# Interleaving 28 shared-expert units with the channel-mix steps, in a new order of TensorE's work

## The reference, cut to what matters

```
h  = layernorm(x) * (1 + ca) + sa
# time mix: h normalized again, mixed with the row before it
r, k, v = sigmoid(xr @ Wr), xk @ Wk, xv @ Wv        # 512 x 512 each
x2 = h + (r * wkv(k, v)) @ Wout
# channel mix: x2 normalized, mixed with the row before it
x3 = x2 + sigmoid(xr2 @ Wr2) * ((relu(xk2 @ Wk2) ** 2) @ Wv2)
x  = x + ga * x3
h3 = layernorm(x) * (1 + cb) + sb
shared = (silu(h3 @ Wsg) * (h3 @ Wsu)) @ Wsd        # hidden size 704
scores = softmax(h3 @ Wrouter); the best 2 of 8 experts per row
routed = sum over the two: score * (silu(h3 @ Wg[e]) * (h3 @ Wu[e])) @ Wd[e]   # hidden 352
out = x + gb * (shared + routed)
```

## Time and profile before

| | |
|---|---|
| time, three runs | 1895.73, 1896.31 (median), 1900.86 us |
| span of the profiled execution | 1895.5 us |
| PE busy | 1742.5 us, 92% of the span |
| DVE busy | 1312.1 us, 69% |
| ACT busy | 707.1 us, 37% |
| POOL busy | 619.4 us, 33% |
| DMA | 351.39 MB, mean 185 GB/s |

### The profile page before, as it was taken

The page is one execution under the profiler, slowest core; times in us unless marked ns, Lnnn a source line. Parts: engine busy times, 40 slices in busy tenths (PEclk is TensorE's granted clock), DMA queues, the critical chain, the costliest instruction groups (busy, mean ns, idle before and its releaser), DMA issues.

```text
span 1895.5 us, 29657 instructions
## 1 busy us (share of the span) xinstructions
PE 1742.5 (92%) x9060; PEld 1509.1 (80%) x9060; DVE 1312.1 (69%) x2333; ACT 707.1 (37%) x1118; POOL 619.4 (33%) x755
## 2 busy tenths in 40 slices
PE   4599999998899899997779999999999999999997
PEld 0488888886677777776678998999999999988886
DVE  4898999983798888886632227666666666655555
ACT  2344444442443434343211115454545454522222
POOL 0343333322577777776216420000000000034442
PEclk8699999999888888888798999999999999999999
DMA  8333343333855454543448735767676767666553
GB/s 332 101 116 120 120 120 120 120 99 116 299 170 183 172 190 166 187 161 128 139 167 285 260 111 199 248 228 251 228 253 225 256 221 254 229 198 178 182 181 101
DMA packets 147870, 351.39 MB, mean 185 GB/s; under 512 B 20793, under 2 KB 20793, under 8 KB 142321
## 3 DMA queue, kind: packets, MB, share of 16 engines
q1 hardware_dynamic: 117136, 263.26, 41.7%
q0 software_dynamic: 19456, 67.12, 10.8%
q10 hardware_dynamic: 11232, 20.45, 2.8%
HBM read 225.95 MB, written 124.83 MB: 185 GB/s over the span
## 4 chain that ended last, share of the span: by engine, by line
PE 72%; DVE 16%; issue 5%; DMA 3%; ACT 2%; POOL 1%; DVEq 1%; SPq 0%; ACTq 0%; POOLq 0%
PE bank L451 17%; PE bank L453 17%; PE bank L452 17%; DVE mix L1345 5%; PE bank L1828 5%; PE bank L1830 5%; PE bank L1829 5%; PE bank L462 3%; PE bank L1804 2%; DVE xh L1330 2%; DMA stage<-in_w_k 1%; DVE raw L1630 1%; DVE h_hl L1400 1%; PE bank L1758 1%; DVE raw L1625 1%
## 5 line engine op out<-in xcount | busy, mean ns | idle before, releaser
L451 PE MATMUL bank<-gu_hi,ex_x_hl 128*128 128x352 f32 x1136 | 381.6, 336 | 24.2 <-DMA ex_x_hl<-h_turned 22.3
L453 PE MATMUL bank<-gu_hi,ex_x_hl 128*128 128x352 f32 x1136 | 370.0, 326 | 0.0
L452 PE MATMUL bank<-gu_lo,ex_x_hl 128*128 128x352 f32 x1136 | 367.3, 323 | 0.0
L1541 DVE TENSOR_TENSOR hid<-bank,sg_t 128x352 f32<-128x352 f32 x142 | 74.5, 525 | 298.3 <-ACT sg_t L1071 294.5
L882 POOL DMA_DIRECT2D ex_x_hl<-h_turned x32 | 18.4, 575 | 691.1 <-PE bank L453 659.9
L451 PEld LDWEIGHTS bank<-gu_hi,ex_x_hl 128*128 128x128 f32 x1136 | 215.5, 190 | 25.2 <-issue 14.5
L1071 ACT ACTIVATE sg_t<-bank 128x352 f32<-128x352 f32 x142 | 65.9, 464 | 417.7 <-PE bank L453 390.9
L452 PEld LDWEIGHTS bank<-gu_lo,ex_x_hl 128*128 128x128 f32 x1136 | 215.6, 190 | 0.0
L453 PEld LDWEIGHTS bank<-gu_hi,ex_x_hl 128*128 128x128 f32 x1136 | 214.7, 189 | 0.0
L1828 PE MATMUL bank<-dn_hi,hid_hi 128*128 128x512 f32 x426 | 169.0, 397 | 9.7 <-DVE hid_lo L1545 9.1
L1830 PE MATMUL bank<-dn_hi,hid_lo 128*128 128x512 f32 x426 | 168.7, 396 | 0.0
(11 more groups left out here) (215 smaller groups left out, 4051.8 us busy)
## 6 DMA issues: line engine op xcount, KB each, us to landing
raw<-in_ex_gu SPq DMA_DIRECT2D x39, 1408.0 KB, 6.6
expert_in_rows<-zero_rows SPq DMA_DIRECT2D x32, 624.0 KB
raw<-in_ex_dn SPq DMA_DIRECT2D x39, 512.0 KB, 7.6
ex_x<-expert_in_rows SPq DMA_DIRECT2D x78, 256.0 KB, 2.7
expert_out_rows<-y_rows ACTq DMA_DIRECT2D x78, 256.0 KB, 2.8
h_rows<-h_t SPq DMA_DIRECT2D x64, 256.0 KB, 3.2
h_turned<-h_hl POOLq DMA_DIRECT2D x32, 512.0 KB, 4.4
ex_x_hl<-h_turned POOLq DMA_DIRECT2D x32, 512.0 KB
```

The lines of the kernel that those rows point to most:

```text
L451: pe.matmul(acc, act_hi[i], w_hi[i], start=(i == 0), stop=False)
L452: pe.matmul(acc, act_hi[i], w_lo[i], start=False, stop=False)
L453: last = pe.matmul(acc, act_lo[i], w_hi[i], start=False, stop=(i == chunks - 1))
L1541: dve.tensor_tensor(hid[:, half, 0:F], PS_U[half][:, 0:F], sg_t[:], ALU.mult).then_inc(u_vec.sem_of["hid"], 1)
```

## The change

The shared expert's units are spread over three places in another way, and the channel step is ordered anew:

- Tiles 0 to 13 (`FU = 14`, part FUSED) have their 28 units inside the channel steps 6 to 33, one unit per step (`LAG = 6`). EARLY keeps tiles 14 to 22 (18 units, `SPLIT = 23`), LATE tiles 23 to 31 (18 units). ROUTED is unchanged.
- tk and cv work on the step's own tile, t3 and the router on the tile two before. Gate and up stand between r2 and k2, t3 ahead of tk, the router ahead of cv. Several buffers that were double are single (`xm2_hi`, `xm2_lo`, `h3_hl`), and PSUM banks are shared (t2 with t3, k2 with cv, the logits with the up half).
- x2 = h + o is made on DVE in the time-mix stage straight from PSUM (`x2_of`); o's store and load, ACT's copy and POOL's add go.
- The modulation rows of the channel stage are loaded per tile (`load_mod`); the residual of the fused tiles goes through DRAM (`load_rs`, `store_rs`) and comes back to SBUF in EARLY, by 14 loads of which at most two are under way, ahead of the first `load_rows`.
- The shared weights are split in hi and lo in channel steps 1 to 5 (`shared_hi`, `shared_lo`) instead of around the stage's end. Turned rows are stored and loaded by ACT's queue instead of POOL's.
- The routing's six pieces stand at units 0 to 5 of EARLY (0, 1 and 3 to 6 before); the scatter's ring has 4 buffers. In LATE one combine stands after every unit.

```diff
-SPLIT = NT // 2
-SC = 3
+FU = 14
+SPLIT = 23
+LAG = 6
+SC = 4
...
-EARLY = Part(0, SPLIT, 0, None)
+FUSED = Part(0, FU, 0, None)
+EARLY = Part(FU, SPLIT, 0, FUSED)
...
 # SP, behind the channel stage
+            for n in range(2, SC):
+                load_scattered(n)
...
+            sp.wait_ge(route_done, 1)
+            for first in range(2):
+                load_expert(ROUTED.tile(first))
+            for n in range(SC, NT):
+                load_scattered(n)
+            sp.wait_ge(rs_out, 16 * FU)
+            for n in range(FU):
+                if n >= 2:
+                    sp.wait_ge(fb_in[n % 2], 16 * (n // 2))
+                sp.dma_start(base[:, n, :], xres_d[n * P:(n + 1) * P, :]).then_inc(fb_in[n % 2], 16)
...
 # POOL
-            sweep(pool, NT, *in_turn((diff_2, -1), (x3, 2), (rstd_3, 3), (rstd_2, -3), (gated, 2), (xres, 2), (x2, -4),
-                                     (store_turned, 5)))
+            lead, _, channel_step = in_turn((diff_2, -1), (x3, 1), (gated, 1), (xres, 1), (rstd_3, 1), (rstd_2, -3))
+            with_units(pool, lead, channel_step)
...
 # ACT
-            sweep(act, NT, *in_turn((sr2_of, 0), (k2hi, 1), (h3hi, 4), (mix2_hi, -1), (k2_of, 0), (h2T_of, -2),
-                                    (first_gu0, 1), (first_gu1, 2)))
+            lead, _, channel_step = in_turn((sr2_of, 0), (hidhi_of, LAG), (silu_of, LAG), (k2_of, 0), (mix2_hi, -1),
+                                            (h3hi, 2), (k2hi, 0), (store_turned, 2), (h2T_of, -2), (shared_hi, 0),
+                                            (first_turned, 0))
+            with_units(act, lead, channel_step)
...
 # DVE, time mix and channel mix
+            def x2_of(t):
+                dve.wait_ge(*rw_pe.done(t.n, "out"))
+                dve.wait_ge(hin_in[t.p], 16 * t.half + 16)
+                dve.tensor_tensor(hin_t[:, t.p, :], PS_O[:], hin_t[:, t.p, :], ALU.add).then_inc(x2_vec.sem, 1)
...
+            def shared_lo(t):
+
+                if t.pair is None and 2 <= t.n <= 3:
+                    i = t.n - 2
+                    dve.wait_ge(sh_split_hi, i + 1)
+                    dve.tensor_tensor(flat(gu_lo[i][:]), flat(gu_in[i][:]), flat(gu_hi[i][:]).bitcast(F32),
+                                      ALU.subtract).then_inc(sh_split_lo, 1)
...
-            sweep(dve, NT, *in_turn((pads, 1), (y_of, 2), (logits_out, 5), (first_col_2, -1), (stats_3, 3), (stats_2, -3), (moments_3, 3), (xhat_2, -2),
-                                    (moments_2, -3), (mixes_2, -1), (h3lo, 4), (k2lo, 1), (mix_lo_2, -1), (scaled_3, 3),
-                                    (h3_of, 3), (first_shared, 4)))
+            lead, _, channel_step = in_turn((logits_out, 3), (first_col_2, -1), (mixes_2, -1), (fused_hidlo, LAG),
+                                            (stats_3, 1), (moments_3, 1), (fused_hid, LAG), (mix_lo_2, -1), (h3lo, 2),
+                                            (k2lo, 0), (scaled_3, 1), (h3_of, 1), (stats_2, -3), (moments_2, -3),
+                                            (xhat_2, -2), (fused_base, LAG), (pads, 0), (shared_lo, 0), (y_of, 0))
+            with_units(dve, lead, channel_step)
...
 # PE, channel mix
-            sweep(pe, NT, *in_turn((r2, 0), (tk, 1), (t3, 4), (k2, 0), (t2, -2), (router, 4), (cv, 1)))
+            def fused_up(v):
+                if not in_fused(v):
+                    return
+                if v.back(1).real():
+                    w = v.back(1)
+                    if w.back(1).real():
+                        pe.wait_ge(*u_vec.done(w.back(1).n, "hid_lo"))
+                    pe.wait_ge(*u_vec.done(w.n, "hid"))
+                    rows_turned(w.p)
+                if v.p == 0:
+                    pe.wait_ge(sf_in, 16 * v.half + 16)
+                if v.pair is None and v.n < 2:
+                    pe.wait_ge(sh_split_lo, v.n + 1)
+                rows_up(PS_G[0], 0, 1, v.p)
+                pe.wait_ge(*lg_vec.done(v.back(LAG - (LAG + 3)).n, "copied"))
+                rows_up(PS_U[0], F, 1, v.p).then_inc(u_pe.sem_of["up"], 1)
+
+            def fused_down(v):
+                if not in_fused(v) or not v.back(1).real():
+                    return
+                w = v.back(1)
...
+                pe.wait_ge(*u_vec.done(w.n, "hid_lo"))
+                rows_down(w.p, w.p == 0, w.p == 1)
+
+            lead, _, channel_step = in_turn((r2, 0), (fused_up, LAG), (k2, 0), (t3, 2), (tk, 0), (fused_down, LAG),
+                                            (router, 2), (cv, 0), (t2, -2))
+            with_units(pe, lead, channel_step)
...
 # DVE, LATE
+                    q = 2 * (n - SPLIT - 1) + half
+                    if 0 <= q < NT // 2 - 1:
+                        combine(q)
```

More of the change, by code:

```diff
@@ L225, in build @@
[L225 to L229, removed]
-        for w in W2:
[L231 to L268, removed]
-            gate_sign, gate_neg = xh[0:B, :], flat(diff1[0:B, :, :])
@@ L634, in _, with first_x2 @@
-            wait_a1(sp)
-            sp.wait_ge(zero_out, 16 * NT)
-            def later_ho(t):
-                if t.pair is not None or t.n >= 4:
-                    load_ho(t)
+                    sp.wait_ge(*xh2_vec.done(t.back(2).n, "xhat"))
+                sp.wait_ge(x2_out[t.p], 16 * t.half + 16)
+                sp.dma_start(x2_t[:, t.p, :], x2_d[bass.ds(row, P), :]).then_inc(x2_in[t.p], 16)
+            def first_x2(t):
+                if t.pair is None and t.n == NT - 2:
+                    sp.wait_ge(*lnh_vec.done(NT - 1, "h"))
+                    for n in range(2):
+                        load_x2(Tile(None, n, NT))
@@ L1051, in _ @@
[L1051 to L1061 removed]
+                act.activation(flat(h3_hl[:, 0]), PS_T23[:], ACT.Copy).then_inc(t3_act.sem, 1)
@@ L1165, in _ @@
-            sweep_part(act, LATE, 1, 1, late_step)
+            for n in range(SPLIT, NT):
+                t = LATE.tile(n)
+                for half in range(2):
+                    if n == SPLIT:
+                        expert_hi(Tile(None, NJ + 1, NJ + 2), half)
+                    hidhi_before(*LATE.before(t, half))
+                    silu(LATE.unit(t, half), bank_of(LATE, half))
+                    if half and n + 2 < NT:
+                        load_turned(LATE, n + 2)
+                    if n == SPLIT:
+                        store_y(ROUTED.last(), half)
+                    else:
+                        first_product(2 * (n - SPLIT - 1) + half)
@@ L1168, in _ @@
+            hidhi_before(LATE, LATE.last(), 1)
+            for q in range(2 * (NT - SPLIT - 1), NT // 2):
+                first_product(q)
         @block.vector
@@ L1658, in _ @@
+            hidlo(LATE, LATE.last(), 1)
+            base_of(LATE, NT - 1)
+            dve.wait_ge(*base_vec.done(NT - 1, "base"))
+            combine(NT // 2 - 1)
         @block.tensor
@@ L1747, in t3 @@
             def t3(t):
+                pe.wait_ge(*h2T_act.done(t.n + 3 if t.pair is not None or t.n + 3 < NT else NT - 1, "h2T"))
                 if t.back(1).real():
@@ L1870, in _ @@
             sweep_part(pe, ROUTED, 1, 1, routed_step)
-            def late_step(t):
-                if t.only(NT):
-                    turn_hid(LATE, LATE.last(), 1)
-                    down(LATE, LATE.last(), 1)
-                if not t.real():
-                    return
+            for n in range(SPLIT, NT):
+                t = LATE.tile(n)
                 for half in range(2):
```

952 lines of the change are left out of this document (516 added, 436 removed).

## The result

The changed kernel takes 1952.34 us (median of 4 runs, 1949.06 to 1954.96) against 1896.82 us before: ratio 1.0293, 95% interval [1.0272, 1.0313]. The forecast was 1896, no change, with a range to 1940: wrong, and on the slow side. The profiled execution has a span of 1947.3 us, 51.8 more than before.

What follows compares the result with a forecast made beforehand. PE, busy 92%, bounds the kernel, DVE the channel step. From 1895.5 us, channel stage -26.4, EARLY +19.4, ROUTED +2 and LATE +4 sum to -1; with 0.8 for the median, 1896, no change; range 1862 to 1940.

Steps and rivals of the forecast that it cites:

- PE has 18 units: 113 us, plus 7 ... ready at S + 120: EARLY: PE's 18 units take 113 us plus 7 for waits at the start, bounds 0 and 20.
- a second chain: EARLY: routing, scatters, residual loads and experts' rows in series, rows ready 152 us after its start; EARLY +19.4.
- the four rivals: Alternative outcomes: clock falls, 1938, 0.20; xhat late, 1924, 0.10; better handover, 1868, 0.22; PE at its own pace, 1857, 0.03.
- The fused step: Channel step with a unit: 18.2 us, of which 1.5 is waiting, 1.06 of it at the transposes of k.
- Rival A: Channel stage: waits make PE's granted clock fall once per fused step, 1.6 us each, 42 in all; 1938, chance 0.20.
- rival B: Channel stage: xhat takes 1.40 us beside POOL and t2 waits, 15 to 42 us in all; 1924, chance 0.10.
- Channel stage: Units filling PE's slack there make it 30.3 us less, of which the start takes 3.9 back: -26.4.
- 95 + 11.2: Channel steps 0 to 5: 84 us, plus 11 for splitting shared weights; then about 11.18 from r2 to k's transposes.
- done long before: Channel step: the eight mixes (3.18 us) finish ahead of their use and cost nothing.
- The table loads: ACT in fused steps: sigmoid and silu alternate, two loads a step, costed at nothing.
- The way into ROUTED: EARLY: routing ends 43 us after its start, tile 4's row lands at 60.5, experts' rows are ready at 152.
- LATE: Last shared-unit stage: one combine after every unit makes some steps 1.7 us late; +4 us, bounds 0 and 14.

Runs made afterwards that it cites:

- 1: Changed kernel with PE's list for EARLY as a loop of two tiles instead of written out; 1951.22 us, ratio 1.0294.
- 7: Changed kernel with each scatter moving 256 floats of a row instead of 512, as many scatters; 1951.36 us (one run).
- 5: Two runs of the changed kernel: scatter ring of 3 buffers instead of 4, 1940.14 us; POOL paced by the landing of scatters two tiles before, 1938.68 us.
- 8: Changed kernel with a small POOL fill ahead of each tile's two scatters, no wait for landing; 1933.07 us, ratio 1.0205.
- 3: Changed kernel with POOL's scatter held until the gate and up products of EARLY's last unit; 1988.43 us (one run).
- 9: Changed kernel with POOL paced by the landing of scatters two tiles before and the 14 residual loads behind ROUTED; 1928.35 us, ratio 1.0174.
- 2: Kernel before with PE's list for EARLY written out tile by tile instead of as a loop; 1898.64 us, ratio 1.0013.
- 6: Kernel before with a scatter ring of 4 buffers instead of 3 and SP's list for EARLY written out; 1906.79 us, ratio 1.0053.

## Why the prediction was wrong

**The step that failed** is "PE has 18 units: 113 us, plus 7 ... ready at S + 120". I took the units in EARLY to run at their own pace beside the scatters, as the earlier trace rows shows them in the kernel before, and summed the scatters, the residual loads and the rows as a second chain that only meets PE at ROUTED's start. With S for EARLY's start, PE was ready at S + 190 (1268.7 - 1079.05): of the 70 us more, 59 are waits beside the scatters, 9 the slower pace at the lower clock, and some 2 waits at the start. The runs show why: beside scatters that come each 1.27 to 1.32 us PE's signals are late and PE stands for some 60 us (1, 7, and the kernel after); beside scatters with gaps it stands for 1 to 2 us (5) or 18 (8), beside none for none (3). Both my rows for scatters were at hand, and the sum even needed POOL to run without waits ("two per tile 2.6 to 2.7"); that this had not happened in the kernel before for longer than eight scatters, and so that its effect on PE was unknown, was the bound I should have set. None of the four rivals had it.

**What else came out.**
- The fused step was right in its wait at the transposes of k (1.06 against 1.06), t2 without a wait, and PEclk 1.00. That 18.43 comes so near to 18.2 is partly luck: PE's own work was 17.4 (18.43 - 1.06) instead of 16.7, and the other 0.4 of the 1.5 of waits didn't come. Rival A is refuted by the clock; rival B didn't come about (xhat took 0.52).
- Channel stage, 10 us less gain than forecast. From the first r2 (475.80) to the transposes of k in step 6 (595.57) it took 119.8 where 95 + 11.2 were summed, 13.6 more: the six steps without a unit took 102.1 instead of 95, and step 6 from its r2 (577.93) 17.6 instead of 11.2. The 25 periods behind it took 461.0 instead of 455, 6 more. The start came 6.6 earlier than the 482.4 of the forecast, and from the last such transposes (1056.55) to EARLY it took 22.5 instead of 25.7. In step 6 PE waits for the first turned rows of a unit, which I had at nothing, and its matmuls then run at the lower clock (0.49 us instead of 0.32). In the steps without a unit the eight mixes take 5.19 us, not 3.18, and start late behind POOL's difference. I costed them at nothing, as "done long before"; in a step without a unit nothing covers them. With POOL idle they took 2.19. PE's wait in step 6, and DVE of the kernel after with POOL idle and in a step without a unit:

```profile
584.90 0.66 PE L507 MATMUL bank<-gu_hi,ex_x_hl 128*128 128x352 f32 x1 [3.93 <-DMA ex_x_hl<-h_turned]
```

```profile
478.91 2.19 DVE L1421 SCALAR_TENSOR_TENSOR mix<-diff,vecs,h2T 128x128 f32<-128x128 f32 x8 [3.93 <-POOL diff L911]
...
523.74 3.09 DVE L1497 TENSOR_TENSOR gu_lo<-gu_in,gu_hi 128x2816 fp32r<-128x2816 f32 x1
...
529.62 5.19 DVE L1421 SCALAR_TENSOR_TENSOR mix<-diff,vecs,h2T 128x128 f32<-128x128 f32 x8 [1.84 <-POOL diff L911]
```

- The table loads cost nothing, as forecast, though they stand behind the wait. By the figure of the Trainium skill ("ScalarE: Activation LUTs", section "What ACT_TABLE_LOAD costs") a switch would be 2.66 us; here each took 1.28 and the activation followed at once.
- The way into ROUTED: routing took 49.5 to the first scatter instead of 43, the row of tile 4 came at S + 73.5 instead of S + 60.5 (two experts' weights ahead of it), the residual loads took the 20 us of the forecast, and the rows could have been there at about S + 165 (the issue at 1240.64 and some 3 us to land) instead of S + 152. With PE's waits taken away (5) this chain does set the start of ROUTED, at S + 176 with pacing: the forecast's mechanism, 24 us longer. Of the residual loads' 20 us only 10 were on the path (9), the rest lay beside the last scatters; I had put them wholly behind.
- LATE: +9.0 where +4 was taken, within the bounds of 0 and 14.

**What stays open.** Why a gapless run of POOL's scatters delays PE's signals. It isn't the layout of PE's code (1, 2), nor the traffic or the bytes (6, 7), and a small gap takes most of it away (8). Whether it is POOL's own work on the scatters or the number of packets that PE's signals wait for was not told apart. The kernel before was never brought to the gapless state (6), so it isn't shown that nothing else of the change is needed for the waits; the loads of turned rows on ACT's queue don't make them alone, since those stand in 5 too.

## What to carry to other kernels

When an edit speeds up one engine's issue of DMAs, treat what runs beside it as unpriced, not as hidden: look in the trace for a stretch where that pace was already held for as long, and if there is none, put a bound on it. A wait called "issue" or "remote" on several engines at once is read by setting the signal's sender beside its receiver: here the matmul had ended 48 us before silu was told. And a stage that fits units into another's waits should be priced by the new order's own step without units (17 us here) and the first step with one (26.1) as much as by the later steps.

## What the runs showed of the hardware

Beside indirect scatters issued by POOL each 1.27 to 1.32 us, with full or half rows, ACT learned of a finished product of PE 48 us late (65 in run 1: 1167.33 to 1232.00), and PE stood inside a product for 2.5 us at a time; at 1.47 us per scatter some 18 us of such waits were left of 60, and at 1.53 with a wait for landings about 2. At as much DMA traffic (315 GB/s) and no more than eight scatters in a row it was 3.5 us. Eight mixes on DVE took 5.2 us beside POOL's work, 3.18 in a step of the kernel before, and 2.19 with POOL idle.
